# Layer 1's experts: rows fetched by node number, sums one expert later, and the folding of attention vectors moved to layer 1's attention

## The reference, cut to what matters

```
k = min(max(int(l * C / e), 1), l)          # 625 * 2 / 8 = 156 nodes for each expert
S = jax.nn.softmax(x @ Wg, axis=-1)         # share of each expert in each node
G, I = jax.lax.top_k(swapaxes(S, 1, 2), k)
ex = jnp.take_along_axis(x[:, None], I[..., None], axis=2)        # the chosen rows
hmid = gelu(einsum('bekh,ehf->bekf', ex, W1) + b1)                # 512 -> 1024
out = einsum('bekf,efh->bekh', hmid, W2) + b2                     # 1024 -> 512
new_x = zeros_like(x).at[arange(b), I].add(G[..., None] * out)
```

## Time and profile before

| | us |
|---|---|
| median of three runs | 1905.63 |
| lowest, highest | 1895.75, 1907.18 |
| profiled execution | 1906.03 |
| its span in the trace | 1904.3 |
| TensorE busy | 1706.0 (90%) |
| VectorE busy | 797.0 (42%) |
| ScalarE busy | 485.1 (25%) |
| POOL busy | 109.5 (6%) |
| mean granted clock of TensorE | 0.936 |

### The profile page before, as it was taken

How to read it: one execution, slowest core, us unless ns; L and a number is a source line. 1 busy time by engine, 2 the same in 40 slices (tenths; PEclk the granted TensorE clock), 3 DMA queues, 4 the chain that set the end, 5 groups by cost and what they waited for, 6 DMA issues and landing times. The chain is left out here.

```text
span 1904.3 us, 26482 instructions
## 1 busy us (share of the span) xinstructions
PE 1706.0 (90%) x9046; PEld 1045.1 (55%) x9047; DVE 797.0 (42%) x2054; ACT 485.1 (25%) x953; POOL 109.5 (6%) x174
## 2 busy tenths in 40 slices
PE   6888989999999799997999999998679999789973
PEld 3345564575456599994677656654223333265532
DVE  6664376721324546665534245331011111322554
ACT  2011224420120222221654135112123223221220
POOL 0011000000000003231000000000000000110000
PEclk9788999999999799997999989989889999799996
DMA  5131136200300546972000210175990897140000
GB/s 151 61 113 33 45 97 235 57 3 1 111 39 0 221 168 209 302 223 64 22 19 5 100 50 28 45 313 226 428 415 7 358 424 295 31 149 1 0 1 27
DMA packets 67989, 241.62 MB, mean 127 GB/s; under 512 B 13212, under 2 KB 16915, under 8 KB 60491
## 3 DMA queue, kind: packets, MB, share of 16 engines
q1 hardware_dynamic: 54133, 214.48, 30.1%
q0 software_dynamic: 13776, 26.10, 4.5%
HBM read 233.40 MB, written 7.11 MB: 126 GB/s over the span
## 5 line engine op out<-in xcount | busy, mean ns | idle before, releaser
L101 PE MATMUL psum<-ahead_arena 125*125 125x257 f32 (+2 forms) x720 | 219.1, 462 | 4.5 <-DVE ahead_W L2333 3.4
L101 PEld LDWEIGHTS psum<-ahead_arena 125*125 125x125 f32 (+1 forms) x720 | 131.5, 189 | 82.4 <-issue 66.5
L715 DVE TENSOR_SCALAR a0e_ring<-a0e_node,a0e_key 125x625 f16 x198 | 70.4, 390 | 75.1 <-PE psum L520 69.5
L101 PE MATMUL psum<-a_W,1_xn_turned 128*125 128x512 f32 x200 | 94.9, 625 | 0.0
L518 PE MATMUL psum<-a0e_ring,a0e_tables 125*128 x198 | 72.7, 421 | 21.0 <-DVE a0e_ring L715 13.1
L2680 PE MATMUL psum<-ahead_arena,ahead_W 128*32 128x256 f32 x960 | 79.5, 386 | 3.6 <-DMA ahead_arena<-in_L_ffn_W 3.6
L101 PE MATMUL psum<-a_W,a0l_H 128*125 128x512 f32 x190 | 81.9, 592 | 0.7 <-issue 0.7
L2660 PE MATMUL psum<-ahead_arena,ahead_W 128*32 128x256 f32 x960 | 62.3, 402 | 20.3 <-DVE ahead_W L2906 13.0
L2911 DVE COPY ahead_W<-psum 32x512 f32<-32x512 f32 x30 | 20.4, 679 | 135.6 <-PE psum L2667 135.6
L101 PE MATMUL psum<-e_xgT,e_W 128*128 128x156 f32 x512 | 69.2, 296 | 0.4 <-issue 0.4
L2704 PE MATMUL psum<-ahead_arena,ahead_W 128*32 128x512 f32 x480 | 61.4, 630 | 9.1 <-DMA ahead_arena<-in_L_ffn_W 4.6
(11 more groups left out here) (626 smaller groups left out, 2938.8 us busy)
## 6 DMA issues: line engine op xcount, KB each, us to landing
ahead_arena<-in_L_ffn_W SPq DMA_DIRECT2D x56, 2048.0 KB, 17.2
e_W<-in_L_ffn_W SPq DMA_DIRECT2D x16, 2048.0 KB, 14.4
1_xn_turned<-half_shares SPq DMA_DIRECT2D x16, 256.0 KB, 8.7
e_stage<-in_L_gnn_W SPq DMA_DIRECT2D x8, 512.0 KB, 8.1
ahead_arena<-in_L_gnn_W SPq DMA_DIRECT2D x2, 2048.0 KB, 10.3
a_W<-in_L_gnn_W SPq DMA_DIRECT2D x3, 1024.0 KB, 5.2
a_qkv<-half_shares SPq DMA_DIRECT2D x11, 256.0 KB, 3.3
a_W<-in_L_ffn_w_down POOLq DMA_DIRECT2D x1, 2816.0 KB, 16.1
```

What stands on the lines that cost most here:

```text
L101: last = nc.tensor.matmul(bank[0:rows, at:at + cols], lhs, rhs, start=(n == 0), stop=(n == len(terms) - 1))
L715: nc.vector.tensor_scalar(ring[:, bass.ds(at, 1), 0:NODES].rearrange("p a n -> p (a n)"), node[:, :], key[:, k, bass.ds(t, 1)], None, ALU. ...
```

## The change

The experts 0 and 1 (`BY_PRODUCT = 2`) are gathered by products as before. For experts 2 to 7:

- `pick(e)` on VectorE writes the places in 16 bits (Pb) instead of P; only the last expert's P is still made, by `choose(7)` in turn 4, for `turn_places`.
- `find(e)` on TensorE multiplies Pb with two columns, row number and tile number of each node: ten 16-bit products of two columns, into one bank of VectorE's. `number(e)` on VectorE makes tile * 125 + row of it, as int32.
- `fetch(e)` on POOL fetches the 156 normalised rows by these numbers, with two indirect DMAs, from a copy of xn in DRAM (`xn_rows`), which SP writes once behind the weights of experts 0 and 1.
- `gather(e)` is eight transposes of the fetched rows, which ScalarE copies in two parts. It stands behind output(e-1), directly ahead of hidden(e).

Ranking runs three experts ahead instead of two. `combine` comes one turn later, and stands ahead of the output copies. `fold_attention` leaves the experts and stands in layer 1's attention, in 24 half units: ten after the k pieces, one each after q pieces 2 and 5 and after the kv copies, four among the outputs, seven behind the `graph` sums. Its loads stand on SP there, among the others; chunks of the second matrix pass through four buffers.

```diff
@@ layer1_attention, VectorE
+                def fold_attention(halves_of_chunks):
+                    for _ in range(halves_of_chunks):
+                        unit, half = len(folded) // 2, len(folded) % 2
+                        layer, k = unit >= CH, unit % CH
+                        if len(folded) == 0:
+                            dve.wait_ge(sem["gat_landed"], 16)
+                            dve.wait_ge(sem["att1_landed"], 32)
+                        if len(folded) == 2 * CH:
+                            dve.wait_ge(sem["att2_landed"], 32)
...
+                        for hd in (2 * half, 2 * half + 1):
...
+                                nc.vector.tensor_tensor_reduce(
+                                    out=junk[:, w, :], in0=weights[:, cols], in1=att[:, int(layer), w, cols], scale=1.0,
+                                    scalar=0.0, op0=ALU.mult, op1=ALU.add,
+                                    accum_out=ahead.wa[:, unit, n:n + 1]).then_inc(done.sem, 1)
...
                 for n in range(len(pieces)):
+                    if n == TILES:
+                        put_high(n - 1)
+                        fold_attention(10)
                     cut_low(n)
-                    if n:
+                    if n and n != TILES:
                         put_high(n - 1)
+                    if n in (TILES + 2, TILES + 5):
+                        fold_attention(1)
...
+                fold_attention(1)
                 mean(0)
                 for t in range(TILES):
                     add_out(t)
                     if t + 1 < CH:
                         mean(t + 1)
+                    if t != CH - 1:
+                        fold_attention(1)
...
                     if t >= TILES - 2:
                         norm.on_vector(dve, t - (TILES - 2), last)
+                    if t < TILES - 1:
+                        fold_attention(2 if t < TILES - 2 else 1)
@@ layer1_attention, SP
+                get(ahead.W1[:, :, :], w_view(d["L2_gnn_W1"]), "gat_landed")
+                for layer in range(2):
+                    for w, name in enumerate(["src", "dst"]):
+                        get(att[:, layer, w, :], bcast(d[f"L2_gnn_att_{name}{layer + 1}"], 128), f"att{layer + 1}_landed")
+                    if not layer:
+                        get(W[:, :, :], w_view(d["L1_gnn_W"]), "w_landed")
+                        get(b[:, :], bcast(d["L1_gnn_b"]), "b_landed")
+                for k in range(CH):
+                    sync.dma_start(stage[:, k, :], w_view(d["L2_gnn_W2"])[:, k, :]).then_inc(stage_landed[k], 16)
                 sync.dma_start(c.saved_AT, c.AT[:, :, :]).then_inc(sem["weights_saved"], 16)
@@ layer1_ffn, TensorE
                 def gather(e):
+                    if e < BY_PRODUCT:
...
+                    pe.wait_ge(sem[f"rows_in{e % 2}"], 32 * (e // 2))
+                    for i in range(2):
+                        for_act(("gather", e, i), [turned(128, TOPC, rows_in[:, e % 2, i, chunk(k)],
+                                                          c.ident[0:TOPC, 0:TOPC], at=128 * k) for k in range(CH)])
+                def find(e):
+                    pe.wait_ge(sem["picked"], e - BY_PRODUCT + 1)
+                    for_dve(("find", e), [product(TOPC, [(Pb[:, e % 2, t, i * TOPC:(i + 1) * TOPC], numbers[:, t, :])
+                                                         for t in range(TILES)], 2, at=2 * i) for i in range(2)])
...
                 gather(0)
+                spread(2)
                 hidden(0)
                 for e in range(EXP1):
-                    if e + 2 < EXP1:
-                        spread(e + 2)
-                    if e + 1 < EXP1:
-                        gather(e + 1)
+                    if e + 2 in range(BY_PRODUCT, EXP1):
+                        find(e + 2)
+                    if e + 3 < EXP1:
+                        spread(e + 3)
                     if e == last_expert:
                         turn_places()
+                    if e + 1 < BY_PRODUCT:
+                        gather(e + 1)
                     output(e)
+                    if BY_PRODUCT <= e + 1 < EXP1:
+                        gather(e + 1)
                     if e == last_expert - 1:
                         turn(e)
                     if e + 1 < EXP1:
                         hidden(e + 1)
                     if e != last_expert - 1:
                         turn(e)
@@ layer1_ffn, VectorE
+                def number(e):
+                    got_numbers = take(("find", e))[0:TOPC, 0:4].rearrange("p (i w) -> p i w", w=2)
...
+                    nc.vector.tensor_scalar(found[:, e % 2, :, 1], got_numbers[:, :, 1], float(ROWS), None, ALU.mult)...
+                    nc.vector.tensor_tensor(found[:, e % 2, :, 0], got_numbers[:, :, 0], found[:, e % 2, :, 1], ALU.add)...
+                    nc.vector.tensor_copy(index[:, e % 2, :], found[:, e % 2, :, 0]).then_inc(sem["indexed"], 1)
...
                 for e in range(EXP1):
-                    if e + 2 < EXP1:
-                        order(e + 2)
-                        choose(e + 2)
+                    if e + 2 in range(BY_PRODUCT, EXP1):
+                        number(e + 2)
+                    if e + 3 < EXP1:
+                        order(e + 3)
+                        pick(e + 3)
+                    if e + 3 == last_expert:
+                        choose(last_expert)
+                    if e >= 2:
+                        combine(e - 2)
                     for k in range(CH):
                         nc.vector.tensor_scalar(oT[:, k, :], take(("output", e, k))[:, 0:TOP1], b2[:, e, k:k + 1], None,
                                                 ALU.add).then_inc(sem["vector_freed"], 1)
-                    if e:
-                        combine(e - 1)
-                    if 1 <= e < last_expert:
-                        fold_attention(2 * e - 2)
-                        fold_attention(2 * e - 1)
+                combine(last_expert - 1)
@@ layer1_ffn, POOL
+                def fetch(e):
+                    gp.wait_ge(sem["indexed"], e - BY_PRODUCT + 1)
+                    if e >= BY_PRODUCT + 2:
+                        gp.wait_ge(sem["scalar_filled"], for_scalar.nth(("gather", e - 2, 1)))
+                    for i in range(2):
+                        nc.gpsimd.indirect_dma_start(
+                            out=rows_in[:, e % 2, i, :], out_offset=None, in_=c.xn_rows,
+                            in_offset=bass.IndirectOffsetOnAxis(ap=index[:, e % 2, i:i + 1], axis=0)).then_inc(
+                            sem[f"rows_in{e % 2}"], 16)
+                gp.wait_ge(sem["xn_stored"], 16)
+                fetch(2)
                 for e in range(last_expert):
-                    gp.wait_ge(sem["chosen"], e + 1)
+                    if e and e + 2 < EXP1:
+                        fetch(e + 2)
                     gp.wait_ge(sem["scalar_freed"], for_scalar.nth(("turn", e, 1)))
```

More of the change, by code:

```diff
@@ L1124, in _, with layer1_attention @@
                 gp.dma_start(down[:, :, :], w_view(d["L0_ffn_w_down"])).then_inc(sem["down_landed"], 16)
[L1127 removed]
+def layer1_attention(core, c, d, ahead):
     nc = core.nc
@@ L1146, in layer1_attention @@
         u = sb("u", [ROWS, 2, DIM])
+        att = sb("att", [128, 2, 2, GAT_DIM])
+        stage = sb("stage", [128, CH, GAT_DIM])
+        junk = sb("junk", [128, 2, GAT_HID], BF16)
         signal = signals(nc, ctx, "a1_")
@@ L1319, in add_out @@
                             sem["divided"], 1)
+                folded = []
+                def fold_attention(halves_of_chunks):
[7 more added lines that the diff above has]
+                            dve.wait_ge(sem["att2_landed"], 32)
+                        if layer and not half:
+                            dve.wait_ge(stage_landed[k], 16 * (unit // CH))
+                        weights = stage[:, k, :] if layer else ahead.W1[:, k, :]
+                        start = done.count
+                        for hd in (2 * half, 2 * half + 1):
+                            cols = slice(hd * GAT_HID, (hd + 1) * GAT_HID)
+                            for w in range(2):
+                                n = w * GAT_HEADS + hd
+                                nc.vector.tensor_tensor_reduce(
+                                    out=junk[:, w, :], in0=weights[:, cols], in1=att[:, int(layer), w, cols], scale=1.0,
+                                    scalar=0.0, op0=ALU.mult, op1=ALU.add,
+                                    accum_out=ahead.wa[:, unit, n:n + 1]).then_inc(done.sem, 1)
+                                if done.up() > start + 1:
+                                    dve.wait_ge(done.sem, done.count - 1)
+                        dve.wait_ge(done.sem, done.count)
+                        nc.vector.engine_nop().then_inc(sem["att_folded"], 1)
+                        folded.append(unit)
                 for a, e in HALVES:
@@ L1396, in layer1_ffn @@
         got = sb("got", [ROWS, 2, TILES, DIM])
-        att = sb("att", [128, 2, GAT_DIM])
```

(45 more changed lines are left out.)

77 lines of the change are left out of this document (46 added, 31 removed).

## The result

The kernel after the change takes 1891.12 us in the median of twelve runs (1884.99 to 1897.75), the kernel before 1904.83 in the twelve beside them: a ratio of 0.9935 with a 95% interval of 0.992 to 0.9951, or 13.7 us gained where 17.6 were forecast. That is a change within 1%, to which the prediction gave 0.57. The profiled execution took 1891.35 us (span 1889.6) against 1906.03.

What follows compares the result with a forecast made beforehand. TensorE, busy 90% of the span, was taken as the bound. 32.0 - 5.1 - 4.2 - 3.9 - 0.7 + 2.2 - 1.9 - 0.8 = 17.6 us gained, giving 1888 us, range 1881 to 1901.

Steps and rivals of the forecast that it cites:

- signs of being wrong: Loop clock under 0.98, row transposes waiting for DMA, q waiting for VectorE, or ten thin products over 1.1 us.
- Gathers, row transposes, finds, stalls: Expert loop: gathers gone +32.0, row transposes -5.1, finds -4.2, new wait for ScalarE's copy -3.9, stalls gone +2.2 us.
- start-of-the-loop term: Ahead of the loop: ranking expert 2 moves there, and the first find waits 0.6 us; -0.7 us.
- rival 3: Thin work (row transposes, finds) is cheap and the tail short: 23.5 us gained, 1882; chance 0.12.
- DMA, "cost nothing, but this is the thinnest cover": Loop: 6.1 MB in 20.7 us, 295 GB/s, costs nothing, as a turn with 301 GB/s held its pace.
- POOL in the loop, "cost nothing": Loop: POOL's 14.0 us and two more fetches make 17.2 of 20.7 us per turn, so no cost.
- Rival 1: POOL's queue becomes the bound: 1.6 us lost a turn, 8 in all, at the tail; 1896; chance 0.15.
- the tail: End of the expert stage: POOL's store and fetches gain 3.0 us where TensorE gained 4.94; -1.9 us.
- rows land 8 us before they are used: Loop: fetched rows land some 8 us before their transposes, so POOL's added fetches cost nothing.
- Folding in the attention, 0.8 forecast: Layer 1's attention: only the folding half after tile 3's norm isn't covered, delaying the block's end; -0.8 us.
- the others fall in gaps that hold them: Layer 1's attention: folding halves beyond the first ten fit VectorE's gaps or are made up by the next piece, except one.
- rival 4: The clock falls at gaps between matmuls: 1911, or 1939 if each turn loses a phase; chance 0.09, dear form 0.05.

Runs made afterwards that it cites:

- the kernel with the early fetch: Changed kernel, but POOL issues the fetch of expert e+3's rows between the store of expert e's rows and the wait for it; 1886.04 us, ratio 0.9923.

## Why the prediction was right or wrong

The time fell into the range, and TensorE was the bound as forecast; but errors of opposite sign stand behind the 13.7 us, and part of the agreement is luck: in the two profiled executions, the stages that were changed show 7.7 us of the 17.6, and the medians differ by 6 more in a way that stays open (see the sum below). One of the prediction's own signs of being wrong came true: row transposes waited for DMA.

*Gathers, row transposes, finds, stalls.* Right in kind and too dear in size. By the prediction's terms the loop, counted from its first find, should have gained 32.0 - 5.1 - 4.2 - 3.9 + 2.2 = 21.0 us; the 0.7 for the start lie ahead of that. Undisturbed it gained 180.02 - 155.32 = 24.7. The finds take 0.37 us each, not 0.70: 2.0 less for six. That is 0.037 us for a 16-bit product of 78 columns loaded, 0.55 of what the f32 row of 125 columns gives by columns alone; why it is so much less, no run tells. The spread behind a find takes 0.08 more than before. Row transposes and the wait for ScalarE take 1.33, not 0.86 + 0.77 = 1.63: 1.5 less for five, of which hidden gives back 0.4 (8.56 to its turn, not 8.48), and 0.2 for expert 7. There, in the kernel with a quarter of the weights, the turn follows at once, and the eight transposes take 0.63 us start to start, 0.079 each, between the two bounds. One spread of 0.54 has left the loop, which the start-of-the-loop term charged ahead of it and never gave back; the five others give back 0.3 of it. The turn of expert 6 gets back 0.7, not 0.5. Together 3.7, which is what was missing: mostly the thin work of rival 3.

*DMA, "cost nothing, but this is the thinnest cover".* This is the step that failed. The rate was as forecast, 296 GB/s at a share of 0.98 in one turn, and the row with 301 GB/s had held its pace. But a sum of bytes tells whether the engines can carry them, not how long one small transfer takes among them. In that turn of the earlier trace rows, about as full (0.97 against 0.98), POOL had issued its last fetch 11 us before the store went, and the store took 6.06 us. With fetched rows still under way beside the weights, such a store took 10.2 to 11.7.

*POOL in the loop, "cost nothing".* It falls with the step above: 17.2 us of issues counted the store wait as before. With 11.5 us in place of 5.73, a turn is 22.3 us and no longer fits in 20.2. Rival 1 named this mechanism (chance 0.15), with 1.6 us lost per turn and 8 in all; measured are 11.3. It also put the loss in the wrong place. I had it come out at the tail, where the part behind the first `sum` product grew by 0.3 us only (1.9 forecast; VectorE waits 2.39 for its last rows, not 4). It came out inside the loop, at what waits for POOL: 1.68 + 4.50 + 2.35 = 8.5 us of waits, 1.8 of slower hidden products and 0.6 of slower transposes, 10.9 of the 11.3. The prediction said that rows land 8 us before they are used. For experts 2, 4, 6 and 7 they were in time; for 3 and 5 they were not, since the fetch stands on POOL's queue behind a store wait and five other fetches, and is then awaited for 12 us or more itself.

*Folding in the attention, 0.8 forecast.* It cost 2.9 in the profiled execution, and 2.2 in the kernel with this part alone. The half behind tile 3's norm cost 5.52 - 4.91 = 0.6, as forecast. The other was missed: "the others fall in gaps that hold them" was argued from VectorE's idle time, and the half ahead of the last scaled output did fall in a gap of VectorE, but TensorE's next product needed the bank which that output frees. That is 1.23 us. What the rest of the 2.2 to 2.9 is, no row tells. With both halves moved one place the attention is back at 129.5 to 129.6.

*The clock, rival 4.* It didn't come about by the work that the change put there: with 1.9 us of turn, find and spread and 1.3 of row transposes and wait in every turn, the quiet turns and the whole loop of two experiments have clock 1.00. The Trainium skill, "TensorE: Matmul & The Clock Gate" (HAM oscillation), says that waits for DMA between bursts drop the clock again and again. The trace agrees with it for real waits only: behind the wait of 4.50 us the piece has 0.76 and hidden takes 1.8 us more, behind the one of 1.68 hidden takes its 8.72. It isn't the length of the wait alone, since in the kernel with the early fetch an output took 10.40 behind one of 1.51. The Trainium skill's part on PE-mode transpose had me fear that transposes would count as idle; in this loop, with 8 + 8 + 5 of them in every turn, no row shows that.

*The sum.* 17.6 forecast, + 3.7 for thin work and the spread, - 11.3 for late stores and rows, + 1.6 for the tail, - 2.1 for the attention, and - 1.8 for the part before the loop (2.5 longer, 0.7 forecast, see the last section) is 7.7: what experts and attention show in the two profiled executions, 10.55 - 2.9. The other 7 us between these two executions lie in code that is the same (4.9 ahead and 2.1 behind). The medians differ by 13.7, 6 more than 7.7. About 2 of that is the part before the loop, which was a long one in this trace (in three kernels with this change, where the products for the gate took about as long as before, it was 0.3 to 0.4 longer than before). What the rest is stays open; the code behind the experts, which no version alters, took 1019.8 to 1029.4 us in the executions with right results.

## What to carry to other kernels

A transfer that is small but waited for is priced by its time under the load that the change brings, not by the sum of bytes. A row as full as the new load is no proof if other transfers make it full: look at what is still under way when the waited-for one goes, here fetches beside weights, and ask of each such wait what is queued behind it on its engine. Work set into an engine's idle time is free only if the next thing that it delays isn't a buffer that another engine waits for. An undisturbed version of the stage (here a quarter of the weights) gives in one run the length it could have, and so the size of the loss.

## What was not expected of the hardware

The 40 thin products for the gate, the same in all these kernels, took 5.74 us in some executions and 8.54 in others. First their line in the changed kernel and the clock of that stretch, then both in the kernel with a quarter of the weights, which is no different up to there:

```profile
640.97 8.54 PE L101 MATMUL psum<-e_Wg,1_xn_turned 128*125 128x8 f32 x40 [0.77 <-ACT 1_xn_turned L1666]
...
640.97:648.00 7.03, 7.03 (x34) 7.03 (x34) 0.00 (x0) 1.16 (x1) 0.00 (x0) 0.50 1.04 391
```

```profile
644.06 5.75 PE L101 MATMUL psum<-e_Wg,1_xn_turned 128*125 128x8 f32 x40 [0.77 <-ACT 1_xn_turned L1666]
...
644.06:649.00 4.94, 4.94 (x37) 4.94 (x38) 0.00 (x0) 1.15 (x1) 0.00 (x0) 0.80 1.04 367
```

Behind the idle time between two stages the clock is at 1.2 GHz (0.50) and comes back to 2.4 at a moment that differs from one execution to the next. So the whole part ahead of the loop was 42.4 to 42.5 us in four profiled executions of kernels with the new experts and 40.2 to 40.6 in six. One trace of before and one of after can differ by 2 us there for no reason of the change.

An indirect fetch keeps POOL for 0.94 us with 78 rows and for 1.20 with 125.
